# Four whole-width VectorE products of a selective-scan stage, made in quarters with one operand in PSUM

## The reference, cut to what matters

```python
xz = x @ in_w
xm, z = jnp.split(xz, 2, axis=-1)                # 256 channels each
xc = jax.nn.silu(causal_conv(xm) + cb)
Bp, Cp = jnp.split(xc @ xw, 2, axis=-1)          # 64 states each
dt = jax.nn.softplus(xc @ dw + db)
A = -jnp.exp(alog)
def step(h, inp):                                # over the 640 positions
    xt, dtt, Bt, Ct = inp
    h = jnp.exp(dtt[..., None] * A) * h + (dtt * xt)[..., None] * Bt[:, None, :]
    return h, jnp.einsum('bdn,bn->bd', h, Ct) + dvec * xt
y = ys * jax.nn.silu(z)
x = layer_norm(y @ ow + x)
```

## Time and profile before

| what | value |
|---|---|
| median of 3 runs | 6471.19 us (6469.46 to 6471.34) |
| the profiled execution's own time | 6495.84 us |
| its span, from the first to the last instruction | 6494.1 us |
| busy share of the span | DVE 88%, POOL 73%, PE 60%, ACT 50%, PEld 35% |
| scans of the Mamba loop, first and last start | 1549.5 and 5673.1 us |
| DMA | 29.6% of 16 engines' span, 106 GB/s of HBM traffic |

### The profile page before, as it was taken

How to read it: one execution, slowest core, us unless ns; L and a number is a source line. 1 busy time by engine, 2 the same in 40 slices (tenths; PEclk the granted TensorE clock), 3 DMA queues, 4 the chain that set the end, 5 groups by cost and what they waited for, 6 DMA issues and landing times. The chain is left out here.

```text
span 6494.1 us, 61166 instructions
## 1 busy us (share of the span) xinstructions
PE 3920.4 (60%) x13720; PEld 2254.6 (35%) x13720; DVE 5697.2 (88%) x7312; ACT 3243.8 (50%) x5534; POOL 4760.5 (73%) x3337
## 2 busy tenths in 40 slices
PE   3213412215676776776767767767667676667777
PEld 3102411213343333333433333334333333245556
DVE  3677666765999999999999999999999999967778
ACT  1112211214566656666666666666566665544445
POOL 4362145225999999999999999999999999833334
PEclk9656556657999999999999999999999999987878
DMA  1000000003444444444444444444444444300000
GB/s 26 1 1 11 2 1 1 11 18 116 160 163 168 160 166 165 160 174 160 165 165 160 166 164 161 173 160 165 165 160 166 164 160 170 141 4 2 2 2 2
DMA packets 171496, 695.04 MB, mean 107 GB/s; under 512 B 27970, under 2 KB 34627, under 8 KB 171139
## 3 DMA queue, kind: packets, MB, share of 16 engines
q1 hardware_dynamic: 169608, 688.25, 29.6%
q0 software_dynamic: 1536, 3.14, 0.2%
HBM read 684.77 MB, written 6.55 MB: 106 GB/s over the span
## 5 line engine op out<-in xcount | busy, mean ns | idle before, releaser
L1022 PE MATMUL m_PS<-m_pr,ident 128*128 128x512 f32 (+1 forms) x6144 | 2496.3, 544 | 907.3 <-DVE m_pr L1146 907.1
L806 POOL TENSOR_TENSOR m_hs<-m_u,m_BC 128x1280 f32<-128x1280 f32 x1024 | 2975.9, 2906 | 68.6 <-DVE m_u L1163 68.6
L1138 DVE TENSOR_TENSOR_SCAN m_hs<-m_PS,m_hs 128x640 f32<-128x640 f32 x2048 | 2934.8, 1467 | 5.2 <-POOL m_hs L806 3.0
L863 ACT ACTIVATE m_PS<-m_dt,m_A 128x640 f32<-128x640 f32 x2048 | 1613.3, 794 | 909.9 <-DVE m_hs L1138 896.3
L1022 PEld LDWEIGHTS m_PS<-m_pr,ident 128*128 128x128 f32 x6144 | 1134.9, 195 | 2167.8 <-DVE m_pr L1146 1133.1
L813 POOL TENSOR_TENSOR m_pr<-m_hs,m_BC 128x384 f32<-128x384 f32 x1024 | 1070.1, 1045 | 184.5 <-DVE m_hs L1138 179.9
L1146 DVE TENSOR_TENSOR m_pr<-m_hs,m_PS 128x896 f32<-128x896 f32 x1024 | 1079.8, 1055 | 8.2 <-DVE m_hs L1138 8.0
L270 POOL TENSOR_TENSOR g_prod<-g_hbuf,g_E 128x128 f32<-128x128 f32 (+1 forms) x888 | 471.1, 548 | 832.7 <-ACT g_E L320 636.3
L852 ACT COPY m_PS<-m_BC 128x448 f32<-128x448 f32 x1024 | 546.5, 534 | 155.8 <-DVE m_pr L1146 107.5
L354 PE MATMUL g_TB<-ident,g_nrm 128*128 128x128 f32 x200 | 66.2, 332 | 574.7 <-DVE g_nrm L490 569.9
L557 DVE TENSOR_TENSOR g_accA<-g_accA,g_prod 128x128 f32 x592 | 255.2, 431 | 158.0 <-DVE g_accA L557 122.1
(11 more groups left out here) (241 smaller groups left out, 4435.8 us busy)
## 6 DMA issues: line engine op xcount, KB each, us to landing
m_BC<-m_scr SPq DMA_DIRECT2D x1024, 640.0 KB, 3.8
m_scr<-m_CB SPq DMA_DIRECT2D x32, 160.0 KB, 4.2
m_hs<-in_cwr SPq DMA_DIRECT2D x4, 512.0 KB, 3.9
out<-f_res SPq DMA_DIRECT2D x20, 64.0 KB, 1.5
m_inw<-in_in_w SPq DMA_DIRECT2D x4, 256.0 KB, 4.0
m_dtw<-in_dw SPq DMA_DIRECT2D x4, 256.0 KB, 3.6
m_xw<-in_xw SPq DMA_DIRECT2D x8, 64.0 KB, 3.8
m_outw<-in_ow SPq DMA_DIRECT2D x4, 128.0 KB, 3.4
```

The source lines that it names most:

```text
L806: pool.tensor_tensor(hs[:, g % RH], u[:, p % 2], BC[:, g % UB:g % UB + 1, 0:S].to_broadcast([P, DT, S]), ALU.mult).then_inc(w_ready, 1)
L863: act.activation(half[d], dt_[:, p % 2, d], ACT.Exp, scale=A[:, l, d, n:n + 1]).then_inc(da_ready, 1)
L1022: ins = pe.matmul(Y[:, a:e], ident[:], pr[:, g % RP, a:e], start=False, stop=False, skip_group_check=True)
L1138: v.tensor_tensor_scan(hs[:, g % RH, d, :], half[d], hs[:, g % RH, d, :], 0.0, ALU.mult, ALU.add).then_inc(scan_done, 1)
```

## The change

Each of the four products is cut into NQ = 4 quarters of QW = 320 columns, and each quarter sits in a unit of its own: silu(z) at n = 21 to 24 (GZ), silu(conv) at 25 to 28 (GX), dt at 40 to 43 (SP) and u at 44 to 47 (UP). In each such unit ACT waits for mult(g) (semaphore prod_ready), writes its quarter into bank C (tanh, tanh, logarithm, or for u a plain copy of dt, which is a new instruction), DVE multiplies it from there with the other operand in SBUF, after its scan of the second half, and copy_c(g+1) waits for that product before it fills bank C. So tanh and the logarithm are no longer written to soft over the whole width; abs and exp(-|v|) still are (now n = 38 and 39). Behind the added steps, the others move: B, C and dt projections to n = 29 to 37, the DMA store of B and C from 40 to 45, the second table load from n = 34 to the abs at n = 38, and the layer norm's steps of the last block from 24, 34, 40 to 46, 48, 49 to 48, 49, 50 to 56, 58, 59. In the head the same pieces run in order, and each quarter waits for the one before it. Where DVE multiplies Y by silu(z) at n = 0, it now also waits for that product's four quarters (sz_ready).

```diff
--- before.py
+++ after.py
@@ -646,11 +646,11 @@
     UNITS = NLB * NST
     LAST = LAYERS - 1
 
-    OUT, TR, ZP, CV, BCP, DTP = 1, 6, 9, 13, 25, 28
-    N_TR, N_ZP, N_CV, N_BCP, N_DTP = 3, 4, 8, 3, 6
-    TANHZ, GATEZ, TANHX, GATEX, STORE = 21, 22, 23, 24, 40
-    STATS, RSTD, ABS, EXPA, LNA, DTS, UMUL = 24, 34, 35, 36, 37, 38, 39
-    STEP, SCALE_R, NORM, SCALE, SHIFT = 40, 41, 42, 48, 49
+    OUT, TR, ZP, CV, GZ, GX, BCP, DTP, SP, UP = 1, 6, 9, 13, 21, 25, 29, 32, 40, 44
+    N_TR, N_ZP, N_CV, N_BCP, N_DTP, NQ = 3, 4, 8, 3, 6, 4
+    ABS, EXPA, STORE = 38, 39, 45
+    STATS, RSTD, STEP, SCALE_R, NORM, SCALE, SHIFT = 48, 49, 50, 51, 52, 58, 59
+    QW = W // NQ
     THIRDS = ((0, 224), (224, 448), (448, S))
 
     with ExitStack() as ctx:
@@ -715,8 +715,8 @@
         bcp_ready, bcp_taken, dtp_ready, dtp_taken = sem("bcp_ready"), sem("bcp_taken"), sem("dtp_ready"), sem("dtp_taken")
         out_ready, out_taken = sem("out_ready"), sem("out_taken")
         bc_stored = sem("bc_stored")
-        tanhz_ready, tanhx_ready = sem("tanhz_ready"), sem("tanhx_ready")
-        abs_ready, expabs_ready, soft_ready = sem("abs_ready"), sem("expabs_ready"), sem("soft_ready")
+        tanhz_ready, tanhx_ready, ln_ready, dt_copied = sem("tanhz_ready"), sem("tanhx_ready"), sem("ln_ready"), sem("dt_copied")
+        abs_ready, expabs_ready = sem("abs_ready"), sem("expabs_ready")
         dt_ready, u_ready = sem("dt_ready"), sem("u_ready")
         bc_loaded = [sem(f"bc_loaded{k}") for k in range(UB)]
         w_ready, da_ready, scan_done = sem("w_ready"), sem("da_ready"), sem("scan_done")
@@ -798,7 +798,7 @@
                 def w_unit(g):
                     p, n = at(g)
                     if n == 0:
-                        pool.wait_ge(u_ready, p + 1)
+                        pool.wait_ge(u_ready, (p + 1) * NQ)
                     pool.wait_ge(bc_loaded[g % UB], (g // UB + 1) * 16)
                     if g >= RH:
                         pool.wait_ge(prod_ready, g - RH + 1)
@@ -857,14 +857,14 @@
 
                     def one(d):
                         if n == 0 and d == 0:
-                            act.wait_ge(dt_ready, p + 1)
+                            act.wait_ge(dt_ready, (p + 1) * NQ)
                         if g >= 1:
                             act.wait_ge(scan_done, 2 * (g - 1) + d + 1)
                         act.activation(half[d], dt_[:, p % 2, d], ACT.Exp, scale=A[:, l, d, n:n + 1]).then_inc(da_ready, 1)
 
                     return one
 
-                def pre_take(q, n):
+                def pre_take(q, n, clear=None):
                     l, b = place(q)
                     if TR <= n < TR + N_TR:
                         k = n - TR
@@ -907,36 +907,50 @@
                         d, (a, e) = k // 3, THIRDS[k % 3]
                         act.wait_ge(dtp_ready, q * N_DTP + k + 1)
                         if q >= 1:
-                            act.wait_ge(dt_ready, q)
+                            act.wait_ge(dt_ready, q * NQ)
                         act.activation(zdt[:, d * S + a:d * S + e], C[:, 0:e - a], ACT.Identity, bias=dtb[:, l, d:d + 1]
                                        ).then_inc(dtp_taken, 1)
                         return dtp_taken, q * N_DTP + k + 1
+                    if GZ <= n < GZ + NQ:
+                        k = n - GZ
+                        if k == 0:
+                            act.preload_act_table_set("exp_and_others")
+                        act.wait_ge(z_taken, (q + 1) * N_ZP)
+                        act.wait_ge(*clear)
+                        act.activation(C[:, 0:QW], sz[:, q % 2, k * QW:(k + 1) * QW], ACT.Tanh).then_inc(tanhz_ready, 1)
+                        return sz_ready, q * NQ + k + 1
+                    if GX <= n < GX + NQ:
+                        k = n - GX
+                        act.wait_ge(cv_taken, (q + 1) * N_CV)
+                        act.wait_ge(*clear)
+                        act.activation(C[:, 0:QW], xc[:, k * QW:(k + 1) * QW], ACT.Tanh).then_inc(tanhx_ready, 1)
+                        return xc_ready, q * NQ + k + 1
+                    if SP <= n < SP + NQ:
+                        k = n - SP
+                        act.wait_ge(expabs_ready, q + 1)
+                        act.wait_ge(*clear)
+                        act.activation(C[:, 0:QW], soft[:, k * QW:(k + 1) * QW], ACT.Ln, bias=1.0).then_inc(ln_ready, 1)
+                        return dt_ready, q * NQ + k + 1
+                    if UP <= n < UP + NQ:
+                        k = n - UP
+                        act.wait_ge(dt_ready, (q + 1) * NQ)
+                        act.wait_ge(*clear)
+                        act.copy(C[:, 0:QW], dt_[:, q % 2].rearrange("p d t -> p (d t)")[:, k * QW:(k + 1) * QW]
+                                 ).then_inc(dt_copied, 1)
+                        return u_ready, q * NQ + k + 1
                     return None
 
                 def pre_more(q, n):
                     l, b = place(q)
-                    if n == TANHZ:
-                        act.preload_act_table_set("exp_and_others")
-                        act.wait_ge(z_taken, (q + 1) * N_ZP)
+                    if n == ABS:
+                        act.preload_act_table_set("natural_log_exp_and_others")
+                        act.wait_ge(dtp_taken, (q + 1) * N_DTP)
                         if q >= 1:
-                            act.wait_ge(dt_ready, q)
-                        act.activation(soft[:], sz[:, q % 2, :], ACT.Tanh).then_inc(tanhz_ready, 1)
-                    if n == TANHX:
-                        act.wait_ge(sz_ready, q + 1)
-                        act.wait_ge(cv_taken, (q + 1) * N_CV)
-                        act.activation(soft[:], xc[:], ACT.Tanh).then_inc(tanhx_ready, 1)
-                    if n == RSTD:
-                        act.preload_act_table_set("natural_log_exp_and_others")
-                    if n == ABS:
-                        act.wait_ge(dtp_taken, (q + 1) * N_DTP)
-                        act.wait_ge(xc_ready, q + 1)
+                            act.wait_ge(ln_ready, q * NQ)
                         act.activation(soft[:], zdt[:], ACT.Abs).then_inc(abs_ready, 1)
                     if n == EXPA:
                         act.wait_ge(abs_ready, q + 1)
                         act.activation(soft[:], soft[:], ACT.Exp, scale=-1.0).then_inc(expabs_ready, 1)
-                    if n == LNA:
-                        act.wait_ge(expabs_ready, q + 1)
-                        act.activation(soft[:], soft[:], ACT.Ln, bias=1.0).then_inc(soft_ready, 1)
 
                 def post_take(q, n):
                     l, b = place(q)
@@ -988,11 +1002,12 @@
                         act.activation(x_tok[:, b * TILES + j, :], x_tok[:, b * TILES + j, :], ACT.Identity,
                                        scale=rstd[:, j:j + 1], bias=nmr[:, j:j + 1]).then_inc(x_ready, 1)
 
+                taken = None
                 for n in range(NST):
-                    pre_take(0, n)
+                    taken = pre_take(0, n, taken) or taken
                     pre_more(0, n)
                 act.wait_ge(a_ready, 1)
-                copy_c(0, (dtp_taken, N_DTP))
+                copy_c(0, taken)
                 for g in range(2):
                     for d in range(DT):
                         decay(g)(d)
@@ -1000,7 +1015,7 @@
                     p, n = at(g)
                     if g + 2 < UNITS:
                         decay(g + 2)(0)
-                    taken = pre_take(p + 1, n) if p + 1 < NLB else None
+                    taken = pre_take(p + 1, n, (prod_ready, g + 1)) if p + 1 < NLB else None
                     if p >= 1 and not taken:
                         taken = post_take(p - 1, n)
                     if g + 1 < UNITS:
@@ -1064,7 +1079,7 @@
                     if BCP <= n < BCP + N_BCP:
                         k = n - BCP
                         a, e = THIRDS[k]
-                        pe.wait_ge(xc_ready, q + 1)
+                        pe.wait_ge(xc_ready, (q + 1) * NQ)
                         for d in range(DT):
                             ins = pe.matmul(C[:, 0:e - a], xw[:, l, d, :], xc[:, d * S + a:d * S + e],
                                             start=(d == 0), stop=(d == DT - 1))
@@ -1147,27 +1162,36 @@
                                     C[:, 0:XD].unsqueeze(1).to_broadcast([P, DT, XD]), ALU.mult).then_inc(prod_ready, 1)
 
                 def pre_step(q, n):
-                    if n == GATEZ:
-                        v.wait_ge(tanhz_ready, q + 1)
-                        v.scalar_tensor_tensor(sz[:, q % 2, :], soft[:], 1.0, sz[:, q % 2, :], ALU.add, ALU.mult
+                    dtq = dt_[:, q % 2].rearrange("p d t -> p (d t)")
+                    uq = u[:, q % 2].rearrange("p d t -> p (d t)")
+                    if GZ <= n < GZ + NQ:
+                        k = n - GZ
+                        r = slice(k * QW, (k + 1) * QW)
+                        v.wait_ge(tanhz_ready, q * NQ + k + 1)
```

(28 more changed lines are left out.)

## The result

| | before | after |
|---|---|---|
| median of the runs, same chip | 6470.32 us (4 runs, 6468.07 to 6471.34) | 6353.93 us (4 runs, 6351.82 to 6364.94) |
| profiled execution | 6495.84 us, span 6494.1 | 6352.39 us, span 6350.7 |
| ratio | | 0.9824, 95% interval 0.9807 to 0.9841 |

The kernel became faster by 116.4 us, where 115 was forecast. The two profiled spans differ by more, 143.4 us. Divided at the starts of the first and the last scan: the part ahead of the layers' first product gave -28.8 us (1448.1 to 1419.3), the head +1.0, the loop -114.2 (4123.6 to 4009.4), what follows -1.4. The first part runs the same instructions in both kernels.

The account below looks back on a forecast made before the run. DVE was taken as the bound, at 258.2 us per block. Removed products -228.1, quarters +89, lost cover +18 and head +6.1 make -115 us from the median 6471.2: 6356 us, range 6325 to 6405.

Parts of the forecast that it names:

- Removed: DVE, loop: the four whole products go, two of them waiting for POOL; 228.1 us less.
- Quarters: DVE, loop: 240 quarter products added at 0.37 us each, 89 us more; bounds 80 and 108 us.
- Lost cover: Loop, n = 21, 38 and 48: ACT work no longer covered by long DVE products; 18 us more.
- Ring: Loop units, ACT and DVE handing over bank C: scan covers the quarter's tanh, slack 0.7 and 0.9 us, no quarter waited for.
- ACT late: Rival, loop: copy_c and second decay over a microsecond later; each of 240 units loses 0.25 us, 6416 us; chance 0.12.
- the open ring: Rival, loop units: tanh, product, copy_c, decay not covered by DVE's scan; 1.1 us per unit, 264 us, 6620; chance 0.04.
- Head: Head, without cover: 16 links of ACT, DVE and two handovers take 16.0 us instead of 9.9; 6.1 us more.
- L1174: DVE product with both inputs in SBUF, moved from n = 48 to 58: zero change, upper bound 11 us.
- Sum: Whole kernel: -228.1 + 89 + 18 + 6.1 = -115 us, subtracted from the median 6471.2, giving 6356 us.

Follow-up runs that it names:

- early tables: Changed kernel with both activation-table loads one unit earlier, at the end of ACT's work for n = 20 and 37: 6345.33 us, 0.9807; again on another chip, 0.9815.
- XD 448 and 440: XD: time-axis columns DVE multiplies for both engines, 448 before and in the change. The change, table loads one unit earlier, with 440: 6347.07 us, 0.9812.
- the change with XD 464: Changed kernel with XD = 464 instead of 448, moving 32 columns of h * C per unit from POOL to DVE: 6410.37 us, ratio 0.9865.
- XD 432: Kernel before with XD = 432 instead of 448, moving columns of h * C from DVE to POOL: 6551.72 us, ratio 1.0084.

## Why the prediction was right

**Removed, -228.1.** Right as a number. As a reason it held for about half. I put both waits down to the pair of SBUF inputs, cured by PSUM. For z that is shown at XD = 448: with SBUF quarters one instruction of 4.7 us stays in each block, and with z and dt whole 64 us of the gain are gone. For dt it isn't: its wait is gone in all three kernels that put dt, from SBUF, where POOL's lag is about 0.2 us or less. I had written that x and u "kept their 1.46 and 1.59 us in spite of POOL", and not asked why; the answer, a lag of 0.17 us for x and an idle POOL for u, was in the trace of before.

**Quarters, +89.** 460 to 471 ns against 452, and 4.16 - 3.76 = 0.40 us per unit against 0.37: +96. The estimate of 0.49 us with nothing overlapped, from the Trainium skill (VectorE: DVE Perf Modes, "The TRN2 errata"), is what the trace has for a quarter behind idle time (0.49 us at 2609.88), though the page measured its 150 cycles with operands in SBUF. As a cost of each quarter it isn't borne out: behind a scan a quarter lasts 0.46 us, and the next scan begins 0.07 us before its recorded end (2614.06 + 0.46 against 2614.45), so tiles of 320 cost the kernel 22 us less than by that figure.

**Lost cover, +18.** n = 21: 0.56 us (forecast 0.6); n = 38: 0.44 (0.45); together 8.3 + 6.7 us. Behind n = 48 a unit has 3.91 us, 0.15 above the others (0.1). Sum 17.3. That this is ACT's queue is shown for n = 38 by the early tables; for n = 21 it is read from ACT's timeline.

**Ring.** From the end of L1161 at 2612.74: tanh ends 0.54 later (forecast 0.55), the quarter 1.78 (1.83), copy_c 2.44 (2.4). Slack 0.66 us (0.7). No quarter but the first is waited for, so neither ACT late nor the open ring came.

**Head, +6.1.** The sixteen links have 8.37 + 8.28 = 16.65 us, 6.7 more than before. The whole head grew by only 1.0. The other 5.7 lie in a step that my sum doesn't have, the nine projections of B, C and dt on PE between silu(conv) and the abs. They took 20.0 us before and take 14.4 now. One of them before and the same one now:

```profile
1526.78 1.86 PE L1077 MATMUL m_PS<-m_xc,m_dtw 128*128 128x224 f32 x4 [0.54 <-ACT m_yz L911]
```

```profile
1498.99 1.02 PE L1092 MATMUL m_PS<-m_xc,m_dtw 128*128 128x224 f32 x4 [0.54 <-ACT m_yz L911]
```

TensorE's granted clock was 0.50 (its 1.2 GHz) from 1518 to 1538 us before, and 1.00 (2.4 GHz) from 1496 to 1506.5 us now; PE had stood idle for 7.5 and for 10.3 us ahead of the first projection. All five traces of the changed kernel at XD 448 and 440, with and without early tables, have 14.4 us, the other nine have 20.0, the change with XD 464 among them, whose head is 109.4 us instead of 102.5. Why the clock rose in the one group and not in the other stays open. So the price of the links was right, and that the head cost only 1.0 us is luck.

**L1174, zero.** As L1198 it has 13.9 us (824 to 7060 ns); four runs of 0.8, 1.1, 1.1 and 6.5 before are 9.6. So +4.3, within the bound of 11: at the lag that I had reckoned with (0.37 to 0.38 us, 0.36 before) one of the two quick runs became 4.92 us. The wait of 7.06 us at a lag of 2.5 doesn't fit the rule of the Trainium skill that the port pair is held for one instruction (SBUF — State Buffer, "Who interferes with whom"), as 6.35 in the earlier trace rows didn't.

**Sum.** In the loop: -228.1 + 96 + 17.3 + 4.3 = -110.5, measured -114.2 here and -110.7 with the second profile of the change. A term that the forecast doesn't have makes up the difference: DVE's idle time in front of the unit's product fell from 8.2 to 4.4 us; in the second profile x_tok's product takes 3.7 us more. The forecast had -121 in the loop and +6 in the head, the traces have -114 and +1. That the total came within 1.4 us is therefore partly luck: two misses of 7 and 5 us cancel. To subtract from the median and not from the profiled execution was right: in the traces 28.8 us of the difference lie ahead of the layers, and the loop's terms hold without them. That the 24.65 us lay there too is argued, for the unprofiled runs have no trace.

## What to carry to other kernels

A DVE product with both inputs in SBUF, dropped into a stream where GpSimd works back to back, is cheap or costs several GpSimd instructions, and which of the two is read from one number: how late GpSimd is when the product starts. Cure it where it is cheapest: a PSUM operand for the product that meets a late GpSimd (here z, and dt where the stall at n = 38 is gone; z alone was not run), or some columns moved so that GpSimd doesn't fall behind; doing both pays twice. When some instances of a form wait and others don't, ask why before crediting the form; and take work from the busiest engine only after looking at who gets it (XD 432).

## What the runs showed of the hardware

How long a DVE product with two SBUF inputs takes beside a POOL with more work ready, by POOL's lag at its start, over all kernels here, XD 432 to 464 (the lag runs from the end of the scan to the end of POOL's running L806):

| lag, us | product of 1280 columns | x_tok product of 640 |
|---|---|---|
| up to 0.28 | 1.46 to 1.71 us, always; L813 is stretched to 2.1 to 2.3 | 0.83 to 0.88 |
| 0.36 to 0.40 | 1.80 (11 times) or 5.59 (4 times) | 1.12 to 1.14, or 4.92 to 4.94 |
| 0.62 to 0.79 | 5.8 to 6.0 | 5.3 |
| 1.0 to 1.25 | 6.2 to 6.45 | 5.6 |
| above (1.4 to 3.9) | 6.6 to 9.2 | 6.5 to 8.5 |

Up to 0.28 us the product waits for the end of the running L806 only (1.46 us with no lag, 1.59 at 0.17, 1.71 at 0.28), and L813 waits for it. When POOL is later, the product doesn't get its turn when POOL's running instruction ends: it waits through the next L813 and L806 too, until POOL has nothing ready. That DVE and POOL share a way to SBUF is argued from these durations and from PSUM's effect, it wasn't measured alone; why the boundary lies between 0.28 and 0.62 us, with both kinds at 0.36 to 0.40, stays open. PSUM operands were never held up: 1024 unit products at 1058 ns and 256 quarters at 460 to 471 ns on average, 0.49 us at most, at lags up to 3.7 us.
